# A two-layer transformer on one core: order of turns, scores and value products in the second phase of its cross attention

## What is computed

```python
def _L0_xattn_ref(hidden_states, key_value_states, attention_mask, position_bias, ln_weight, w_q, w_k, w_v, w_out):
    x = _rmsnorm(hidden_states, ln_weight)
    h_q = (x @ w_q.T).reshape(b, lq, H, DH)
    h_k = (key_value_states @ w_k.T).reshape(b, lk, H, DH)
    h_v = (key_value_states @ w_v.T).reshape(b, lk, H, DH)
    score = jnp.einsum('bqhd,bkhd->bhqk', h_q, h_k)
    score = score + position_bias[None]
    score = jnp.where(m, score, -jnp.inf)
    score = jax.nn.softmax(score, axis=-1)
    score = jnp.where(m, score, 0.0)
    attn = jnp.einsum('bhqk,bkhd->bqhd', score, h_v).reshape(b, lq, H * DH)
    return hidden_states + attn @ w_out.T
x = x + _L0_xattn_ref(_layernorm(x), ctx_4096, mask, position_bias, ln_weight, w_q, w_k, w_v, w_out)
```

## Time and profile before

| | |
|---|---|
| median of three runs | 1653.35 us |
| the profiled execution itself | 1653.1 us |
| its span, first to last instruction | 1651.3 us |
| granted TensorE clock over the span | 0.999 |
| busy PE / weight loads / DVE / ACT / POOL | 1633.9 / 1378.0 / 911.3 / 745.3 / 815.1 us |
| PE's waits at line 698 for the copy at line 903 | 4.1 us in 15 |

### The profile page before, as it was taken

One profiled execution on the slowest core, in us unless ns is written; L12 is line 12 of the kernel. 1 busy time (PEld: TensorE's weight loads), 2 busy tenths in 40 slices (PEclk: granted clock), 3 DMA queues, 4 the chain that ended last, 5 costly groups with the idle time before them and its releaser, 6 DMA issues.

```text
span 1651.3 us, 24904 instructions
## 1 busy us (share of the span) xinstructions
PE 1633.9 (99%) x8584; PEld 1378.0 (83%) x8584; DVE 911.3 (55%) x1460; ACT 745.3 (45%) x1930; POOL 815.1 (49%) x628
## 2 busy tenths in 40 slices
PE   9999999999999999999999999999999999999999
PEld 7888888888888888888878887888888888888887
DVE  4621111125566566565668666866657656665675
ACT  5431111115454444454454333666546555654653
POOL 5222212237656556566458775654435544443445
PEclk9999999999999999999999999999999999999999
DMA  8534433322333233233231111010011111010011
GB/s 313 202 137 153 152 130 145 122 87 106 109 105 121 92 107 119 94 119 115 97 145 57 46 52 55 22 70 26 33 39 45 45 39 33 26 33 26 26 52 52
DMA packets 52107, 146.40 MB, mean 89 GB/s; under 512 B 7264, under 2 KB 12000, under 8 KB 51520
## 3 DMA queue, kind: packets, MB, share of 16 engines
q1 hardware_dynamic: 52032, 145.41, 25.1%
HBM read 107.64 MB, written 37.75 MB: 88 GB/s over the span
## 4 chain that ended last, share of the span: by engine, by line
PE 68%; issue 14%; POOL 11%; DVE 3%; ACT 2%; DMA 1%; SPq 0%; POOLq 0%; DVEq 0%; ACTq 0%
PE banks L55 20%; PE banks L57 20%; PE banks L56 20%; PE banks L2043 3%; POOL x_biased L1284 2%; POOL x_probs L1290 2%; POOL wtA_lo L1205 2%; PE banks L2050 1%; POOL wtB_lo L1273 1%; DMA resid<-in_x 1%; POOL resid L198 1%; ACT x_probs L895 1%; POOL rawB L1267 1%; POOL rawB L1264 1%; POOL rawB L1269 1%
## 5 line engine op out<-in xcount | busy, mean ns | idle before, releaser
L2507 POOL TENSOR_TENSOR g_swapped<-g_swapped,rawB 128x512 f32<-128x512 f32 x80 | 103.4, 1294 | 171.5 <-ACT g_swapped L2189 171.3
L1038 DVE COPY c_v_kept<-banks 128x512 f32<-128x512 f32 x64 | 44.2, 691 | 258.6 <-PE banks L57 258.6
L895 ACT ACTIVATE x_probs<-x_probs,x_top 128x128 f32<-128x128 f32 x256 | 99.7, 391 | 120.0 <-DVE x_top L1085 120.0
L1290 POOL TENSOR_TENSOR x_probs<-x_probs,x_inv 128x512 f32<-128x512 f32 x64 | 66.7, 1042 | 175.4 <-DVE x_inv L1094 173.9
L55 PE MATMUL banks<-wtV_hi,g_att_lo 128*128 128x512 f32 x256 | 105.3, 411 | 0.0
L2501 POOL TENSOR_TENSOR g_probs<-g_probs,g_inv 128x512 f32<-128x512 f32 x64 | 67.7, 1081 | 74.6 <-DVE g_inv L2328 74.4
L2337 DVE TENSOR_TENSOR g_turned_by<-banks,rawB 128x512 f32<-128x512 f32 x80 | 55.2, 690 | 87.9 <-ACT g_swapped L2189 87.9
L1104 DVE TENSOR_TENSOR resid<-banks,resid 128x512 f32<-128x512 f32 x128 | 86.4, 684 | 30.0 <-PE banks L57 30.0
L55 PE MATMUL banks<-xT_hi,wtO_lo 128*128 128x512 f32 x256 | 102.8, 402 | 0.0
L2188 ACT COPY g_swapped<-banks 64x512 f32<-64x512 f32 x80 | 46.7, 584 | 121.5 <-PE banks L57 115.1
L56 PE MATMUL banks<-wtV_lo,g_att_hi 128*128 128x512 f32 x256 | 101.3, 396 | 0.0
(11 more groups left out here) (334 smaller groups left out, 5065.1 us busy)
## 6 DMA issues: line engine op xcount, KB each, us to landing
kept_k<-c_k_kept SPq DMA_DIRECT2D x16, 1024.0 KB, 4.0
x_k<-kept_k SPq DMA_DIRECT2D x32, 512.0 KB, 4.0
kept_v<-c_v_kept SPq DMA_DIRECT2D x14, 1024.0 KB, 5.0
x_v<-kept_v SPq DMA_DIRECT2D x28, 512.0 KB, 3.3
rawA<-in_x_wQ SPq DMA_DIRECT2D x16, 512.0 KB, 4.6
rawO<-in_x_wO SPq DMA_DIRECT2D x16, 512.0 KB, 3.4
rawO<-in_g_wQ SPq DMA_DIRECT2D x16, 512.0 KB, 3.5
rawV<-in_g_wO SPq DMA_DIRECT2D x16, 512.0 KB, 3.5
```

Of the source, the lines that this page charges most:

```text
L895: e = nc.scalar.activation(probs[:, b, :], probs[:, b, :], ACT.Exp, bias=top[:, b:b + 1], accum_out=total[:, b:b + 1])
L1290: pool.tensor_tensor(probs[:, part, :], probs[:, part, :], rows, ALU.mult).then_inc(probs_ready, 1)
L2507: pool.tensor_tensor(part, part, sin[:, :].unsqueeze(1).to_broadcast([P, HB, P]), ALU.mult)\
```

## The change

Three engines' lists are written in another order; no instruction is added or taken away.

```diff
@@ tensor, body(g) @@
                 sixth(g)
+                seventh(g)
                 pv(g - 1, 1, 0)
-                seventh(g)
                 pv(g - 1, 1, 1)
                 scores(g, 0, 1)
                 weights_ready("O", CTX_V + g)
-                output(g - 1, 0)
-                output(g - 1, 1)
+                for b in range(HB):
+                    output(g - 1, b)
                 turn(a, 0)
+                turn(a, 1)
                 scores(g, 1, 0)
-                output(g - 1, 2)
-                output(g - 1, 3)
-                turn(a, 1)
                 scores(g, 1, 1)
                 pv(g, 0, 0)
-                output(g - 1, 4)
                 pv(g, 0, 1)
-                for b in range(5, B):
+                for b in range(HB, B):
                     output(g - 1, b)
@@ scalar, body(g) @@
                 probs_turned(a, 0)
+                probs_turned(a, 1)
                 exps(a + 1, 0)
-                probs_turned(a, 1)
                 exps(a + 1, 1)
@@ vector, body(g) @@
                 fourth_sum(g)
+                fifth_sum(g)
                 inverse(a, 0)
-                fifth_sum(g)
                 attn_lo(b_, 0, 1)
                 logits(a, 1)
                 attn_lo(b_, 1, 1)
                 output(g - 1, 0)
                 inverse(a, 1)
-                output(g - 1, 1)
+                for b in range(1, HB):
+                    output(g - 1, b)
                 logits(a + 1, 0)
-                output(g - 1, 2)
-                output(g - 1, 3)
                 logits(a + 1, 1)
                 inverse(a + 1, 0)
                 output(g - 1, 4)
+                inverse(a + 1, 1)
                 output(g - 1, 5)
-                inverse(a + 1, 1)
```

## The result

The changed kernel takes 1646.16 us (median, 1645.92 to 1646.65) against 1653.35 for the one before, measured beside it: a ratio of 0.9956, with a 95% interval of 0.9941 to 0.997. That is 7.2 us less, where 8.1 had been forecast. The profiled execution took 1646.65 us, with a span of 1644.9 and the clock granted in full.

The account below looks back on a forecast made before the run. PE was taken to bound the kernel, busy 1633.9 of 1651.3 us, with a hole at the value products in each body. 15 x 0.54 = 8.1 us less gave 1645.2, range 1643.2 to 1649.0.

Parts of the forecast that it names:

- The hole: PE before the value products, waiting for ACT's late copy: with it gone, each body is 0.54 us shorter.
- The crossings: Between plain and split matmuls, six plain blocks become three: 0.01 us each, 0.4 at most for 45, taken as 0.
- The turn, the copies, output 0: Inputs PE needs in time: cover 1.1 us for half 1's turn, 1.4 and 1.7 for copies, 0.2 at output 0.
- The scores are now done at 738.80, so the logits start at 738.84: DVE's logits of the next head start 0.2 us later than before, with PE's scores starting at 737.74.
- The tight place: DVE's inverse(a+1, 1) before output 5's addition: slips in ahead of POOL's bias, or is held until 746.17, cover 0.05 or none.
- PE asks for it at 746.85: Start of the next body's first_five, needing output 5's addition, which would be done at 746.80 if held.
- Rival 1: Waits return at output 0 or first_five, 0.15 to 0.35 us a body: 1647.3 to 1650.4; chance 0.16.
- The prediction's sign of being wrong: A new row in PE's waits for resid or x_att_lo, with a count of 14 or 15.
- Rival 2: The hole stays at another instruction, ACT's copy or the turn itself being late: 1651 to 1654; chance 0.07.
- rival 3: DVE held too long behind POOL's bias, delaying PE's next body: slower, 1657.0 if the bias ends 0.8 later; chance 0.05.
- Rival 4, the clock: PE's clock at 0.66 from 849 to 853 us behind the stage: 1.5 us either way, used only to widen the range.
- the less favourable reading in the prediction: POOL keeps the port through instructions that follow at once: DVE held 2.4 us in every body, gain 6 us.

Follow-up runs that it names:

- e1: The kernel before with only ACT's two calls swapped, probs_turned(a, 1) ahead of exps(a + 1, 0): 1646.33 us, ratio 0.995.
- e2: The changed kernel with ACT's swap undone, probs_turned(a, 1) behind exps(a + 1, 0) again: 1694.36 us, ratio 1.024.
- e4: The changed kernel with normalise(a - 1, 1) ahead of bias(a, 0) in POOL's list: 1644.11 us, ratio 0.9938.
- e7: The changed kernel with output 5's addition ahead of inverse(a + 1, 1) on DVE, and normalise ahead of bias on POOL: 1645.45 us, ratio 0.9944.
- e3: The changed kernel with DVE's inverse(a + 1, 1) behind the addition of output 5 again: 1645.03 us, ratio 0.9948.
- e5: The changed kernel with three tiny unread additions on POOL between its normalise and its bias: 1644.42 us, ratio 0.9942.
- e6: The kernel before with ACT's swap alone, plus normalise ahead of bias in POOL's list: 1646.39 us, ratio 0.9949.
- e8: The changed kernel measured again, with nothing altered: 1646.9 us, ratio 0.9953.

## Why the prediction was right, point by point

The forecast, 1645.2, is 1.0 us below the 1646.16 measured; the range of 1643.2 to 1649.0 held it, and the side was right.

- **The hole (0.54 a body): right**, alone in e1 at 0.545.
- **The crossings, taken as 0: mis-sized by little.** The bound that I kept at 0.01 for each crossing was the truth: 0.032 for the three fewer in a body, so 0.5 us in 15.
- **The turn, the copies, output 0: covered as worked out.** No idle time stands in the rows from 732.28 to 736.64. The first copy ends at 732.99 + 0.58 = 733.57 and the second at 734.06; the value products ask at 734.94 and, 0.89 later, 735.83. Cover 1.4 and 1.8, forecast 1.4 and 1.7.
- **"The scores are now done at 738.80, so the logits start at 738.84": this step failed.** That is 1.10 behind the start of the scores (737.74). In the changed kernel it is 734.42 - 733.15 = 1.27. The 1.10 does hold for scores that follow value products. Both stand in one body of the changed kernel, PE's scores of `g`'s first and second block:

```profile
720.40 1.06 PE L678 MATMUL banks<-x_k,x_q 128*128 128x128 f32 x8
...
725.87 1.06 PE L678 MATMUL banks<-x_k,x_q 128*128 128x128 f32 x8
```

  and DVE's logits of them:

```profile
721.68 0.69 DVE L1080 TENSOR_TENSOR x_probs<-banks,x_biased 128x512 f32<-128x512 f32 x1 [0.52 <-PE banks L678]
...
726.97 0.69 DVE L1080 TENSOR_TENSOR x_probs<-banks,x_biased 128x512 f32<-128x512 f32 x1 [0.48 <-PE banks L678]
```

  1.27 and 1.10, with PE's recorded durations the same. The kernel before shows it too, behind its first turns (724.98 to 726.25, 1.27), and I hadn't looked there. The turns are not the cause: in body 2, written out ahead of the loop, the logits come 1.09 behind scores that follow turns.

```profile
435.68 1.95 PE L678 MATMUL banks<-x_k,x_q 128*128 128x128 f32 x16
...
436.77 0.69 DVE L1080 TENSOR_TENSOR x_probs<-banks,x_biased 128x512 f32<-128x512 f32 x1 [1.07 <-PE banks L678]
```

  The trace has the reason in the records of DVE's sequencer. In the loop the value that a wait asks for is worked out by an instruction of its own. Behind the turns two of them (lines 1075 and 1077 of the changed kernel, for POOL's bias and for the turn) run only once PE's scores have released DVE, 0.17 and 0.08 ahead of the addition. Behind the value products they have run over 1 us before, and in body 2 there are none. The exponentials, the sums and the multiplication behind them all came 0.17 to 0.19 later. The normalise in front of the bias came where forecast (738.16; 742.75 less the 4.61 us by which this profile is earlier is 738.14), since POOL was busy with `wtB_lo` until then. So the multiplication, which was to come up 0.03 ahead of the bias, came up 0.14 into it. Even without the 0.17 it was a matter of hundredths. In body 2 (DVE, then POOL) POOL's normalise stands 0.07 nearer to the scores, and the multiplication came 0.04 into the bias and was held all the same:

```profile
441.66 2.38 DVE L1091 TENSOR_TENSOR x_inv<-x_inv,x_some 128x4 f32<-128x4 f32 x1
```

```profile
441.62 2.41 POOL L1280 TENSOR_TENSOR x_biased<-normed,row 128x1024 f32<-128x1024 f32 x1
```

- **The tight place: both outcomes were named, and the less favourable came.** "Some hundredths too late" and it is held to the bias's end: so it was, 2.27 us, to 0.02 after POOL's end. I had priced that at 0.05 + 0.11 in 14 bodies (2.2 us); the price was 0.08 at 13 seams, 1.1 us. The addition was done some 0.05 before PE's matmul, as worked out. But "PE asks for it at 746.85" was the wrong moment: what asks is the matmul's weight load, 0.23 earlier, and it was late by some 0.22. That left the matmul on time and the one behind it 0.10 late.
- **Rival 1**, part of it coming back at the seams, happened at half of its least price: 0.08 a body where it said 0.15 to 0.35. It shows as 12 waits of the weight loads for `resid`, not in PE's own list. The prediction's sign of being wrong was a row of 14 or 15 for `resid` in PE's waits, and that list doesn't show it.
- **Rival 2 and rival 3** didn't happen. Rival 3 needed the bias to end 0.54 later than worked out; it ended at 741.56, where 746.17 less 4.61 had been worked out. e2 shows what it would have meant to be wrong about ACT's copy: 41 us, of which some 14 are the clock behind holes of 2.2 us, which I had not considered.
- **Rival 4, the clock**, was worth nothing. The stretch behind the stage that stood at 0.66 is at full clock in the change (842.5 to 846.5 us, granted 1.00). It came and went between the kernels (e1, e4 and e7 have it, e3, e5, e6 and e8 don't), yet `tail` to the feed-forward products is 33.71 to 33.76 in all of them. PE waits there for ACT's and DVE's results in either case, 3.0 us before and 4.4 in the change: what the lower clock costs comes out of these waits.

The sum by these sizes: 0.54 + 0.03 - 0.08 = 0.49 a body, 0.50 measured; over 15, 8.1 + 0.5 - 1.1 = 7.5, and 7.44 in the profile's stage. The medians' 7.2 is 0.3 less, within what two sets of runs of one kernel differ by.

On the port, the Trainium skill (SBUF — State Buffer, Who interferes with whom) calls it "an exclusive lock". The trace agrees on the hold: 2.27 against 0.16 us for the same 128x4 multiplication. Read as kept through instructions that follow at once, which was the less favourable reading in the prediction, e5 speaks against it: there DVE's multiplication is through in 0.20 us while POOL's instructions follow without a break.

The version to keep is e4, the change with the normalise ahead of the bias on POOL: 1644.11 us, 0.9938 (0.9924 to 0.9951) of the kernel before. From body 1 to `tail` it is the shortest, by 0.5 us over e3 and by 0.1 over e5 and e7, which is no more than the marks can tell. The price of its edit, a later bias, has cover: in e4 the logits wait nowhere for it.

## What to carry to other kernels

When an engine waits for a result, read the list of the engine that makes it before reordering anything else: here the copy stood behind four exponentials that were themselves waiting 3.3 us, and one swapped call gave all of the gain. Read the rows of the weight loads too: a wait can stand there and in no row of the matmuls. The larger reordering was worth 0.5 us with that swap, minus 1.1 for a seam, and cost 48 without it, so try the parts alone. And before an instruction that a critical engine waits for is put behind one that shares a port, ask which long instruction can start just ahead of it: some 0.1 us decided between 0.2 and 2.3.

## What the runs showed of the hardware

- A DVE multiplication of 128x4 with both inputs in SBUF takes 0.16 us with POOL idle, 0.20 if it comes up among short POOL instructions that follow each other at once, 2.27 if it comes up 0.14 us into one of 2.40, and 2.38 if 0.04 us into it. When held it ends 0.02 to 0.03 us after POOL's instruction.
- In the loop DVE starts 1.27 us behind the start of a block of scores where two register instructions of its sequencer still stand between PE's release and the addition, and 1.10 where they have run before; in the bodies written out it is 1.09 to 1.10.
- Three blocks fewer between plain and split matmuls save 0.032 us a body, 0.011 a crossing.
- A weight load stands 0.23 us ahead of its matmul and waits for what the matmul waits for. With a result 0.05 us ahead of the matmul but 0.17 behind the load's turn, the next matmul came 0.08 to 0.10 late, with no idle time in PE's rows and 0.26 in the load's.
- Holes of 2.2 us in PE had the clock granted at 0.50 for 3.4 us behind nine of fifteen of them, at 1.6 us each; holes of 0.45 had none.
